# Softmax reciprocals by two square transpositions on VectorE, with a new order of the instruction streams, in a four-batch decoder layer on one core

## The reference, cut to what matters

```python
# attention, on the normalised x
scores = jnp.einsum('bqhd,bkd->bhqk', q, k) * scale
scores = jnp.where(causal[None, None], scores, min_val)
attn = jax.nn.softmax(scores, axis=-1)
ctx = jnp.einsum('bhqk,bkd->bqhd', attn, v)
out = jnp.einsum('bsd,ed->bse', ctx, out_w) + out_b
...
x = x + attention(_layernorm(x), ...)
x = x + quantized_mlp(_layernorm(x), fside, ctx_1024)
x = x + feed_forward(_layernorm(x), ...)
```

## Time and profile before

| | us |
|---|---|
| median of 3 runs | 974.12 |
| lowest, highest | 972.45, 978.3 |
| the profiled execution, first to last instruction | 968.1 |
| TensorE busy, by its profile | 918.0 |
| VectorE busy | 616.9 |
| ScalarE busy | 316.7 |
| GpSimd busy | 313.8 |

### The profile page before, as it was taken

The page is one execution under the profiler, slowest core; times in us unless marked ns, Lnnn a source line. Parts: engine busy times, 40 slices in busy tenths (PEclk is TensorE's granted clock), DMA queues, the critical chain, the costliest instruction groups (busy, mean ns, idle before and its releaser), DMA issues.

```text
span 968.1 us, 13886 instructions
## 1 busy us (share of the span) xinstructions
PE 918.0 (95%) x5333; PEld 678.8 (70%) x5333; DVE 616.9 (64%) x945; ACT 316.7 (33%) x545; POOL 313.8 (32%) x394
## 2 busy tenths in 40 slices
PE   6899999799899999999999999999999999889996
PEld 5775588655468787766778877756778777668885
DVE  3476788578976887766557977754677654432222
ACT  3245521346433234353232243434223331121110
POOL 3556723046831141364200331544014142011110
PEclk9899999799899999999999999999999999999999
DMA  9977545345854733476266433372525446535542
GB/s 313 270 277 293 210 162 130 122 141 205 311 205 123 217 128 132 135 275 247 77 194 176 164 116 143 129 283 104 204 87 177 164 175 214 203 108 188 194 146 93
DMA packets 44967, 175.10 MB, mean 181 GB/s; under 512 B 7197, under 2 KB 10269, under 8 KB 34917
## 3 DMA queue, kind: packets, MB, share of 16 engines
q1 hardware_dynamic: 35780, 114.96, 34.3%
q10 hardware_dynamic: 9120, 59.25, 17.7%
HBM read 127.46 MB, written 33.75 MB: 167 GB/s over the span
## 4 chain that ended last, share of the span: by engine, by line
PE 75%; DMA 7%; DVE 4%; SPq 4%; POOL 4%; issue 3%; ACT 2%; POOLq 0%; DVEq 0%; ACTq 0%
PE ring L1000 12%; PE ring L1001 11%; PE ring L1002 11%; PE slots L1073 4%; PE ring L1236 4%; PE av L1104 4%; PE ring L997 3%; PE slots L1090 3%; PE den L1104 3%; PE slots L1000 3%; PE slots L1002 3%; PE slots L1001 3%; SPq L605 3%; DMA qst<-negm_hl 3%; PE slots L1173 2%
## 5 line engine op out<-in xcount | busy, mean ns | idle before, releaser
L775 POOL TENSOR_TENSOR hd_l<-hd,hd_h 128x512 fp32r<-128x512 f32 x44 | 57.4, 1305 | 293.7 <-ACT hd_h L967 293.6
L1000 PE MATMUL ring<-xT_h,gu 128*128 128x512 f32 x352 | 143.0, 406 | 2.0 <-DMA gu<-gu_parts 1.9
L1002 PE MATMUL ring<-xT_h,gu 128*128 128x512 f32 x352 | 138.3, 393 | 0.0
L1001 PE MATMUL ring<-xT_l,gu 128*128 128x512 f32 x352 | 138.1, 392 | 0.0
L1354 DVE TENSOR_REDUCE negm<-slots 128x1 f32<-128x384 f32 (+3 forms) x176 | 105.9, 636 | 35.2 <-PE slots L1073 34.7
L869 ACT ACTIVATE probs<-slots 128x512 f32<-128x512 f32 (+1 forms) x176 | 90.4, 555 | 95.4 <-PE slots L1090 94.9
L742 POOL TENSOR_SCALAR_AFFINE_SELECT probs<-probs 128x128 f32<-128x128 f32 (+2 forms) x176 | 65.5, 386 | 100.3 <-ACT probs L869 99.8
L1000 PEld LDWEIGHTS ring<-xT_h,gu 128*128 128x128 f32 x352 | 66.5, 189 | 20.8 <-issue 8.5
L1599 DVE TENSOR_TENSOR total<-ring,total 128x512 f32<-128x512 f32 x64 | 44.0, 688 | 51.8 <-PE ring L1002 51.6
L1002 PEld LDWEIGHTS ring<-xT_h,gu 128*128 128x128 f32 x352 | 66.5, 189 | 14.8
L1001 PEld LDWEIGHTS ring<-xT_l,gu 128*128 128x128 f32 x352 | 66.8, 190 | 11.8
(11 more groups left out here) (196 smaller groups left out, 1839.3 us busy)
## 6 DMA issues: line engine op xcount, KB each, us to landing
gu<-gu_parts ACTq DMA_DIRECT2D x42, 1280.0 KB, 5.5
dn<-dn_parts SPq DMA_DIRECT2D x12, 1728.0 KB, 7.4
gu_parts<-gu SPq DMA_DIRECT2D x11, 1280.0 KB, 5.8
qst<-qT_h SPq DMA_DIRECT2D x128, 64.0 KB, 2.8
...
```

What stands on the lines that cost most here:

```text
L775: pool.tensor_tensor(hd_l[:, i, :], hd[:, i, :], hd_h[:, i, :].bitcast(F32), ALU.subtract).then_inc(hd_lo.sem, 1)
L1000: pe.matmul(out_, w_hi_, m_hi_, start=start, stop=False, skip_group_check=True)
L1001: pe.matmul(out_, w_hi_, m_lo_, start=False, stop=False, skip_group_check=True)
L1002: return pe.matmul(out_, w_lo_, m_hi_, start=False, stop=stop, skip_group_check=True)
```

## The change

Three things are changed.

The reciprocals. `den` is the same number on all 32 partitions of a head. After the change DVE transposes `den` in 32x32 squares into `rden`, so that column 0 of each square holds 32 different sums of one head; takes the reciprocal of those 16 columns alone into a new tile `rsum`; and transposes `rsum`, each column repeated 32 times, back into `rden`. The ACT copy of `den` goes away, and the transposition that takes its place is ahead of DVE's copy of `av`. The `context` steps keep only the multiplication.

```diff
@@ sums on ACT
-            def sums(b, g):
-                act.wait_ge(pv_done.sem, pv_done.at(b, 4 * g + 4))
-                if g:
-                    act.wait_ge(cx_ready.sem, cx_ready.at(b, 2 * g))
-                act.activation(rden[:, :], den[:, :], ACT.Copy).then_inc(den_out.sem, 1)
@@ sums and context on DVE
+                dve.transpose(rden[:, :], den[:, :]).then_inc(den_out.sem, 1)
                 dve.tensor_copy(cx[:, g % 2, :], av[:, :]).then_inc(av_out.sem, 1)
+                dve.wait_ge(den_out.sem, den_out.at(b, g + 1))
+                squares = rden[:, :].rearrange("p (c r) -> p c r", r=HD)
+                dve.reciprocal(rsum[:, :], squares[:, :, 0]).then_inc(rsum_ready.sem, 1)
+                dve.wait_ge(rsum_ready.sem, rsum_ready.at(b, g + 1))
+                dve.transpose(squares, rsum[:, :].unsqueeze(2).to_broadcast([P, T // HD, HD])).then_inc(rden_ready.sem, 1)
 
             def context(b, g, hf):
                 cols = slice(T // 2 * hf, T // 2 * (hf + 1))
-                dve.wait_ge(den_out.sem, den_out.at(b, g + 1))
-                dve.reciprocal(rden[:, cols], rden[:, cols]).then_inc(rden_ready.sem, 1)
-                dve.wait_ge(rden_ready.sem, rden_ready.at(b, 2 * g + 1 + hf))
+                dve.wait_ge(rden_ready.sem, rden_ready.at(b, g + 1))
                 dve.wait_ge(av_out.sem, av_out.at(b, g + 1))
                 dve.tensor_tensor(cx[:, g % 2, cols], cx[:, g % 2, cols], rden[:, cols], ALU.mult).then_inc(cx_ready.sem, 1)
```

The order. `TURNS` is a new string with the same letters in another merge. The first line of each:

```diff
 TURNS = (
-    "1111A111AA1A11111111AAA1A11A111A1A11111A111AAAWAA1111111111111111XXX1WW111111111XXXX1111111XXX1111111111AXXXXX"
+    "A4AA6123A2322A3A1AA1A1AA4AAAAW2A3A2X1X11XWXX3X11XXX5XXXXAX1AXX1XWXWW4XXXAAXXXXAAXAAXAAAXXAAAWA1AXAXAWXXAWAW1AW"
```

More of the change, by code:

```diff
@@ new lines @@
+    "XXAAAA41XA3XAAAAAAAWAWAAA15A1AA1XAXA1AXXXA2WAAA1XAAA3XAA3W2AA122A1A2AA1A2A2AAA31AAWAA2AAAAWAAAA2A31AAAAA13W6AA"
+    "AAAAAA1AAWAA1AAA2AWAAAAWAAAWAAWAL1A2LA32LA1L2LLWL4L112A1ALWAALL1124L26WLXX11XX6L1XX121L1LXL3XLLL2XXL4L4XA412AX"
+    "X24922L13LAL215XXX1LX32XX1X1LLL122AXALL1L14X1XLLWLL3LLLA11LLL4171LAA261L2293A2132L162XX1ALL5LAL6X1X45LXLL111AL"
+    "1LAWALAAWAAL31LAA3LAAWW31WAA1A3XAX311X21L3L1L21X6AX11LL1AXLLLAA3ALLA1A1LL4WAXWLLAXWXAXA1A1411AAA121AALLL22AXL3"
+    "X1AXXWXAAA1XAAA21AA1A1AAAL6AAAWLA34AWFAAAAAFAAAFAAAFALLAFAF4ALFA11AAAAFA2AAFAAAAAAFAFA231AF24FA3FAAFAA5FLLALAF"
@@ new lines @@
+    "AALLAFLFFAA1FFAL1F13F1AA41AFLFL1ALAXXFXFFFFLFFF23LFX12WFLFFFFXFFFFL1XFFXF1FF1FLXXFXFLFLFFFLXFLFAXLLFFXALL1LFFF"
+    "XLFXLLF2FFLF1FXAXFFFLFFLLFLFLF2FFAFAFXFFXAXXXFLLAXFFXALFF2AFXLFLFFF4LLFFFXFLFFLFLFFFLFFFALALFAFFXAXFXXXLA1LFAL"
+    "FFAAAFALAFLFFFLLLF1AAA1FLLFALFX1XALFFFXXLLL4FFFLLFAFXFAAAAFXXFAALLFFAFFA1AAAAAXXXXXFAAAFAFFAFFFFAALLFF32FAAAAF"
+    "LLFLA3FLAFFLLFAFLAAAFFLFF1XFFFAFFFFLFLFFFFAFLAAFLFAFAAAFFAFAFLLFAAFLFFAFAAFAAAAFAAAFAAFAAAAAAAALFLFAFFAFFLFAFF"
+    "AAFFFAFLALAAAAALAFFLAALL2LLLFFAAFAFA2FAFAFLAF1FFXXFLFAXFXXFXFFLXFFFFFXXFXXXFXLFAXXFFXFFFLXFAFXXFFFXF1FF1LFFFAL"
@@ L303, in in_order @@
+    "FLFF1LLLFFLFFLFLLFFFFFLFLLFFFLLFLFLFFFFFFFFFFFFFLFLFFFFFFFFFFFLLLFFFFFFFLFLFFFFFLFFFF25FFF9FFFFFFFFFFFFFFF1FFF"
+    "FF8FFFL1F3F1F12FF58FFFFFFFFFFFFFFFFFF1FF2FFF2FFFFFFFFFFFFFFFFFFFFFFFFFFFFFFFFFFFFFFFFFFFFFFFFFFFFFFFF48FFFFFFF"
+    "FFFFFFFFFFFFFFFFFFFFFFFFFFFFFFFFFF2FFFFFFFFFFFFFFFFFFFFFFFFFFFFFFFFFFFFFLLLFLLLLLFFFFFFFFFFF6611FFF5FFFFFFFFFF"
+    "F2F2F")
 def in_order():
@@ L385, in program @@
         rden, cx = sb("rden", [P, T]), sb("cx", [P, 2, T])
+        rsum = sb("rsum", [P, T // HD])
         vT = rden
@@ L978, in _ @@
             steps = {"prep_small": prep_small, "prep_wo": prep_wo, "prep_gu": prep_gu, "prep_dn": prep_dn, "turn1": turn1, "kv": kv,
-                     "q": q, "v": v_, "rows": rows_, "scores": scores, "sums": sums, "split_context": split_context, "tanh": tanh,
+                     "q": q, "v": v_, "rows": rows_, "scores": scores, "split_context": split_context, "tanh": tanh,
                      "s_rows": s_rows_, "round_a": round_a, "round_w": round_w, "copy_a": copy_a, "copy_w": copy_w, "w_row": w_row,
```

18 lines of the change are left out of this document (7 added, 11 removed).

## The result

| | before | after |
|---|---|---|
| median of 20 runs each, us | 974.14 | 977.80 |
| lowest, highest | 968.09, 980.45 | 974.94, 984.15 |
| the profiled execution | 968.1 | 975.5 |

The ratio is 1.0041, with a 95% interval of 1.0023 to 1.0060: the changed kernel is slower by 0.4%. The forecast was 967, faster by 0.7%. Its range (949 to 982) holds the result; its sign is wrong.

The account below looks back on a forecast made before the run. Up to 274.7 us no engine was taken to bound alone, only chained waits; behind it TensorE. 4.7 us ahead at `gate(0, 0, 0)`, then -1.6 and -1: -7.3, a span of 960.8, median 967; range 949 to 982.

Parts of the forecast that it names:

- The reciprocals: On DVE: transpositions of 0.69 us and small reciprocals of 0.18 replace those of 1.744; DVE loses 31 us, 616.9 to 586.
- the dear rival: A transposition runs at the reciprocal's rate, delaying each first context half 5.6 us: +22 us, 989; chance 0.03.
- Item 1: Up to `q(1, 0)`: 91 fewer fills, -9.9 us, some back as waits, DVE relieved by 7.7 us; taken as -7.
- the removed fills stood in waits: Rival: up to `q(1, 0)` the 91 removed fills remain as waits, nothing won there; sum -0.3, 974; chance 0.18.
- Item 2: `q(1, 0)` to `scores(1, 0, 0)`: SP's transfers keep 34 us, with the idle stretch and low clock behind; 0.
- Item 3: To `product1(0, 0)`: 57 matmuls instead of 109, 10 fills instead of 17, -7.2 us by price; taken as -4.
- Items 4 and 5: To `product1(0, 1)`, then to `gate(0, 0, 0)`: 67 and 49 more fills, partly covered by idle time and clock; +1 each.
- Item 6: From `gate(0, 0, 0)` to the end: 160 more fills, +17.4 us, with 16 hidden and 3 of clock; -1.6.
- late fills cost their own time: Rival: behind `gate(0, 0, 0)` none of the added fills hides, +17.4 us there; span 979.8, median 986; chance 0.09.
- The median over the profiled span: Whole kernel: the median of the runs lies 6.0 us above the profiled span (974.1 against 968.1), added to the forecast span.
- the 1 us given to the later reciprocals: The eight groups of batches 2 and 3, hidden under the feed-forward, were given a gain of 1 us in all.
- `q(1, 0)` at 143: Sign of being wrong: `q(1, 0)` still ends at 143 us, where near 137 would show the forecast right.

Follow-up runs that it names:

- recip_only: The kernel after with the order and 471 fills of before, so only the reciprocals are new: median 975.2 us, ratio 1.0038 to before.
- one_filled_wait: Before with 44 more fills in the one wait ahead of `scores(1, 0, 0)`: median 970.2 us, ratio 0.9969 to before.
- recip_one_fill: The new reciprocals in before's order, with 44 more fills ahead of `scores(1, 0, 0)`: median 971.2 us, ratio 0.9954 to before.
- no_middle_fills: After without its 119 fills between `gate(0, 0, 0)` and `turn3(3, 0)`: median 975.5 us, ratio 1.0022 to before.
- no_tail_fills: After without its 72 fills from `turn3(3, 0)` on: median 979.8 us, ratio 1.0082 to before.
- after_to_gate: After's order up to `gate(0, 0, 0)`, then the 18 owed steps and before's order, with the new reciprocals: median 983.0 us, ratio 1.0112 to before.
- after_to_out: After's order up to `out(1, 1)`, then the steps owed and before's order, with the new reciprocals: median 983.1 us, ratio 1.0097 to before.

## Why the prediction was wrong, by its own steps

**The reciprocals: right.** A transposition took 0.717 and 0.711 us where 0.69 was taken, the small reciprocal 0.233 where 0.18 was; VectorE's total is 582.7 where 586 was said. The estimate of 0.53 us and a start, from the rate in the Trainium skill (Vector Engine (DVE) Microarchitecture Reference, "The reshape front-end and per-opcode configuration"), came out with a start of 0.18. The cost of the dear rival (989) is excluded. What the relief of VectorE is worth depends on the order: nothing at full clock in before's (recip_only); 2.8 us there once the head's fills are gone (935.9 to 933.1), which hardly stands out of the scatter and is not seen in the time; 12 us in after's.

**Item 1, up to `q(1, 0)`: -7 said, 0 measured.** This is the first step that failed: the sum had no term for the clock here. Up to `q(1, 1)` the 95 fewer fills are 10.4 us; 6.8 came back at the clock (5.1 us lost in before, 12.0 in after) and some 3 as waits. At full clock the stretch takes 139.0 us in before and 132.2 in after, so the -7 itself, fills less waits, was right. Nor is it an accident of two traces: the four with before's head (before, recip_only, one_filled_wait, recip_one_fill) have 138 to 140 us at full clock and 3 to 10 lost, the five with after's (after, no_middle_fills, no_tail_fills, after_to_gate, after_to_out) 131 to 133 and 12 to 17 lost. The prediction took "a fill stands in a wait or costs its time" for the whole choice, and left out the third: a fill also buys clock. The rival that put item 1 at 0 (974, "the removed fills stood in waits") had the wrong cause for most of it.

**Item 2: 0 said, -1.3 measured: right.** 34.4 us against 34 forecast, by SP's transfers. But its idle part didn't stay: one wait of 5.65 us became 1.8 us plus smaller ones ahead, and the low clock behind it was shorter.

**Item 3: -4 said, -8.6 measured** (19.0 to 10.4). The mechanism was right; the low clock that item 2 let stand was worth 4 us more: 5.7 us of loss in before, 1.7 in after.

**Items 4 and 5: +1 and +1 said, +3.1 and +2.2 measured.** In item 4 the clock took 1.7 us that the sum had at nothing, and TensorE's idle time grew from 1.8 to 2.7 us in spite of 67 more fills. In item 5 the covering worked: idle time 5.3 to 0.7 us, and the 3.4 us of clock are gone. So `gate(0, 0, 0)` came 4.6 us earlier, not 9, with the 4.3 us of matmuls owed: level with before. The two heads spend the same 15.3 and 15.4 us on the clock, in different places.

**Item 6: -1.6 said, some +8 measured.** Behind `gate(0, 0, 0)` before takes 693.4 us and after 705.4, of which 4.3 are the owed matmuls. The second step that failed is "16 us hidden": of the 17.4 us of more fills the clock gave back 5.1 (3 said), and only 4.6 were hidden. The fills of the tail did as said, 134.6 to 134.2 us. The 119 in the middle covered 3.5 of their 13.0 us, while I had 11.8 us of idleness for them from the difference of span and busy time. Most of that difference is no wait in which a fill fits. The rival "late fills cost their own time", given 0.09, is this mechanism; its price of 17.4 was too high, as the tail's were paid for and the clock gave back more than counted. The prediction had after end above before once "over 7.3 + 1.6 us" stayed uncovered; by its own terms item 6 has to pass 5.7 us for that, clock included, and it did.

**The median over the profiled span: +6.0 said, +2.3 measured.** Every run's time is its span plus 1.7 us; the profiled run of before was a quick one of a spread from 968 to 980. The forecast took the luck of one run for a constant. The forecast difference was -7.3, and about +4 came by the medians, +7.4 by the two traces. From -7.3 to +7.4 the misses add up so: item 1 +7.0, item 6 +9.3, items 4 and 5 together +3.3, the 1 us given to the later reciprocals +1, against them items 2 and 3 with -5.9.

Of its signs of being wrong, `q(1, 0)` at 143 came. The waits behind `gate(0, 0, 0)` did shrink, from 25 to 18 us of idle time by the windows, but not by nearly 16; and the longest wait of the tail was 1.4 us, not under 1.
